# The gate of a mixture-of-experts layer fed with raw rows: deviation and mean applied at the logits, setup and stores reordered

## The reference

```python
logits = x_flat @ Wg + bg                    # x_flat: layernorm(x), 4096 x 512; Wg: 512 x 8
probs = softmax(logits); assignments = argmax(probs)
h = gelu(einsum('nd,edh->neh', x_flat, W1) + b1)
eo = einsum('neh,ehd->ned', h, W2) + b2
out = probs[assignments] * eo[assignments]   # one expert per row
x = x + out
```

## Time and profile before

| | us |
|---|---|
| Median of 3 runs | 2038.52 (2037.73 to 2043.76) |
| Profiled execution, its own time | 2036.4 |
| Its span in the trace | 2034.7 |
| PE busy over the span | 1882.0 (92%) |
| Attention stages | about 1657 of the span |
| Front of the expert stage, until the first matmul of the loop | 1657 to 1735.5 |
| Loop of 23 tiles, until the last DVE step | 1735.5 to about 2024 |

### The profile page before, as it was taken

The page is one execution under the profiler, slowest core; times in us unless marked ns, Lnnn a source line. Parts: engine busy times, 40 slices in busy tenths (PEclk is TensorE's granted clock), DMA queues, the critical chain, the costliest instruction groups (busy, mean ns, idle before and its releaser), DMA issues. The chain is left out here.

```text
span 2034.7 us, 34889 instructions
## 1 busy us (share of the span) xinstructions
PE 1882.0 (92%) x10942; PEld 1325.2 (65%) x10942; DVE 1342.8 (66%) x2837; ACT 1140.2 (56%) x2179; POOL 1000.9 (49%) x1147
## 2 busy tenths in 40 slices
PE   2999999999999999999999999999999835999997
PEld 2666666767666766656666666666666324898896
DVE  3666676666667676767575757575765335688886
ACT  3455554555555465655565655565655515787885
POOL 3354555455545555445444545555554434345454
PEclk9999999999999999999999999999999967899999
DMA  6444545545454575445454544535443369322220
GB/s 202 105 101 110 123 103 131 120 107 135 109 132 100 124 182 125 110 113 125 105 125 105 119 111 111 119 87 127 91 103 79 74 201 333 121 78 88 79 86 21
DMA packets 138089, 239.96 MB, mean 118 GB/s; under 512 B 31114, under 2 KB 32434, under 8 KB 137872
## 3 DMA queue, kind: packets, MB, share of 16 engines
q1 hardware_dynamic: 105728, 191.00, 34.7%
q0 software_dynamic: 21968, 46.42, 11.6%
q10 hardware_dynamic: 10240, 0.64, 0.3%
HBM read 115.63 MB, written 50.02 MB: 81 GB/s over the span
## 5 line engine op out<-in xcount | busy, mean ns | idle before, releaser
L535 ACT ACTIVATE attn_probs<-attn_sT 128x512 f32<-128x512 f32 (+3 forms) x1024 | 529.1, 519 | 484.5 <-PE attn_sT L826 480.0
L442 POOL TENSOR_TENSOR attn_probs<-attn_probs 128x512 f32<-128x512 f32 (+2 forms) x384 | 531.1, 1401 | 177.0 <-PE attn_o_ps L841 125.7
L641 DVE TENSOR_REDUCE attn_m_col<-attn_sS 128x1 f32<-128x512 f32 x512 | 342.6, 687 | 193.9 <-PE attn_sS L810 186.1
L826 PE MATMUL attn_sT<-attn_stack 98*128 98x512 f32 (+2 forms) x1024 | 387.6, 390 | 2.8 <-ACT attn_probs L535 2.8
L810 PE MATMUL attn_sS<-attn_stack 97*128 97x512 f32 (+2 forms) x1024 | 369.3, 371 | 14.5 <-DVE attn_m_col L641 6.0
L647 DVE CUSTOM_DVE_ANT_0 attn_sS<-attn_sS,attn_cT_low 128x128 f32<-128x128 f32 x496 | 241.2, 504 | 191.1 <-PE attn_sS L810 187.5
L826 PEld LDWEIGHTS attn_sT<-attn_stack 98*128 98x128 f32 x1024 | 188.0, 189 | 210.1 <-ACT attn_probs L535 115.6
L430 POOL TENSOR_SCALAR_AFFINE_SELECT attn_probs<-attn_probs 128x256 f32<-128x256 f32 x256 | 132.0, 516 | 361.7 <-ACT attn_probs L535 361.6
L841 PE MATMUL attn_o_ps<-attn_probs,attn_V 128*32 128x512 f32 (+3 forms) x2048 | 233.5, 527 | 24.3 <-POOL attn_probs L430 19.6
L810 PEld LDWEIGHTS attn_sS<-attn_stack 97*128 97x128 f32 x1024 | 193.9, 190 | 70.1 <-DVE attn_m_col L641 18.3
L790 PE MATMUL attn_pj<-attn_xT_high,attn_w_high 128*128 128x512 f32 x384 | 153.1, 399 | 3.9 <-DVE attn_w_low L607 3.9
(11 more groups left out here) (190 smaller groups left out, 3765.0 us busy)
## 6 DMA issues: line engine op xcount, KB each, us to landing
attn_stack<-attn_stage SPq DMA_DIRECT2D x672, 128.0 KB, 2.3
attn_rows<-in_x_dram SPq DMA_DIRECT2D x64, 256.0 KB, 4.0
attn_rows<-x_after_self SPq DMA_DIRECT2D x64, 256.0 KB, 4.2
moe_w<-in_L_ffn_W_dram SPq DMA_DIRECT2D x16, 1024.0 KB, 14.9
attn_stack<-attn_stage POOLq DMA_DIRECT2D x96, 128.0 KB, 3.4
x_after_self<-attn_rows SPq DMA_DIRECT2D x32, 256.0 KB, 2.6
x_after_self<-in_L_attn_b_dense_dram POOLq DMA_DIRECT2D x32, 256.0 KB, 5.0
attn_rows<-in_ctx_dram SPq DMA_DIRECT2D x32, 256.0 KB, 3.0
```

The costliest lines, as they stand in the source:

```text
L442: pool.tensor_tensor(total, total, tile_of(n, kb)[:, js, q0:S], ALU.add).then_inc(added, 1)
L535: act.activation(tile_of(n, kb)[:, j, q0:S], sT[:, i % 2, q0:S], ACT.Exp, scale=SCALE).then_inc(exp_done, 1)
L641: dve.tensor_reduce(to, sS[:, k % 2], AX_X, ALU.max).then_inc(s_free, 1)
L826: pe.matmul(sT[:, i % 2, q0:S], stack[0:ROW_MAX + 1, n % 2, 1, j, kb * P:(kb + 1) * P], stack[0:ROW_MAX + 1, n % 2, 0, j, q0:S], start=Tru ...
```

## The change

It touches only the expert stage. Five things are done:

1. PE transposes raw rows as soon as a batch is loaded; `normalize_batch` on ACT and POOL's normalizing of tiles 2 and 3 are gone. Since logits = ((x @ Wg) - mean * sum(Wg)) / deviation + bg, PE once multiplies a matrix of ones by the gate's weights (column sums, `gate_sums`), POOL forms `-mean/deviation * gate_sums + bg` for each batch (`shift`, two steps of 128x32, two batches late), and DVE multiplies the logits by 1/deviation and adds that (one more step in `choose`).
2. POOL's clearing of the gather buffers (`rows`) and its two selects on `carry` move from behind the first batch's layernorm to ahead of it.
3. ACT's order after the last batch is new: all four `store_rec` come ahead of ACT's steps for the route, the first right behind `take_gate` of batch 7. DVE runs `weigh(0)` ahead of `choose(2)`.
4. SP waits for the first tile's gather before it issues the first three loads of b2.
5. SP also waits for DVE's statistics (`g_stats`) before it overwrites a batch.

The diff, cut to its core:

```diff
@@ sync @@
                     if e >= NB:
                         sp.wait_ge(g_full, NB * (2 * (e - NB) + m + 1))
+                        sp.wait_ge(g_stats, N_STATS * (2 * (e - NB) + m) + NB)
...
+            sp.wait_ge(gathered[0], 16 * R)
             for i in range(RING):
                 tile(0, i)
             sp.wait_ge(placed, 4)
             sp.wait_ge(loaded[weight_sem[LENT]], 16)
-            sp.wait_ge(gathered[0], 16 * R)
             load_weights(LENT)
@@ gpsimd @@
+            pool.memset(ones, 1.0).then_inc(const_step, 1)
...
-                for t in range(NB):
-                    if t not in ON_ACT:
-                        pool.tensor_scalar(gx[b][:, t], gx[b][:, t], rec_tok[:, NB * b + t, 1:2],
-                                           rec_tok[:, NB * b + t, 2:3], ALU.mult, ALU.add).then_inc(g_norm[1], 1)
-
-            layernorm(0)
+            def shift(b):
+                ts = slice(NB * b, NB * (b + 1))
+                pool.wait_ge(g_ln, 4 * b + 4)
+                pool.wait_ge(sums_ready, 1)
+                pool.tensor_tensor(logits[:, ts], gate_sums.unsqueeze(1).broadcast_to([P, NB, E]),
+                                   rec_tok[:, ts, 2].unsqueeze(2).broadcast_to([P, NB, E]), ALU.mult).then_inc(shifted, 1)
+                pool.wait_ge(shifted, 2 * b + 1)
+                pool.tensor_tensor(logits[:, ts], logits[:, ts], bg_rows.unsqueeze(1).broadcast_to([P, NB, E]),
+                                   ALU.add).then_inc(shifted, 1)
+
+            pool.memset(rows[:], 0.0).then_inc(const_step, 1)
             pool.wait_ge(route, 4)
             for c in range(2):
                 pool.affine_select(out=carry[:, c, 0:NT], ...)
-            pool.memset(rows[:], 0.0).then_inc(const_step, 1)
-            for b in range(1, B):
+            for b in range(B):
                 layernorm(b)
+                if b >= 2:
+                    shift(b - 2)
+            shift(B - 2)
+            shift(B - 1)
@@ scalar @@
-            normalize_batch(0)
             for b in range(B):
                 take_turned(b, 0)
                 take_turned(b, 1)
-                if b + 1 < B:
-                    normalize_batch(b + 1)
                 if b >= 1:
                     take_gate(b - 1)
                 take_turned(b, 2)
...
                 take_turned(b, 3)
-            for i in range(PAIRS - 1):
-                exponent(i)
+                if b == B - 1:
+                    exponent(0)
+            exponent(1)
             take_gate(B - 1)
+            store_rec(0)
+            exponent(2)
+            store_rec(1)
             exponent(PAIRS - 1)
-            for i in range(2):
+            for i in range(2, PAIRS):
                 store_rec(i)
...
-            for i in range(2, PAIRS):
-                store_rec(i)
@@ vector @@
                 dve.wait_ge(g_gate, 2 * (2 * i + 1) + 2)
+                dve.wait_ge(shifted, 2 * (2 * i + 2))
                 for b in range(2 * i, 2 * i + 2):
-                    op = dve.tensor_tensor(logits[:, NB * b:NB * (b + 1)],
-                                           logits_back(b).rearrange("p (t c) -> p t c", t=NB)[:, :, 0:E],
-                                           over_tiles(bg_rows, NB), ALU.add)
+                    op = dve.tensor_tensor(cand[:, bs], logits_back(b).rearrange("p (t c) -> p t c", t=NB)[:, :, 0:E],
+                                           over_experts(rec_tok[:, bs, 1]), ALU.mult)
                 step(op)
+                stepped()
+                step(dve.tensor_tensor(logits[:, ts], logits[:, ts], cand[:, ts], ALU.add))
...
+            weigh(0)
             choose(2)
             spread_counts(0)
-            for i in range(PAIRS - 1):
+            for i in range(1, PAIRS - 1):
                 weigh(i)
@@ tensor @@
             def turn(b, t):
-                wait_normed(pe, b, t)
+                pe.wait_ge(loaded[b], 16)
...
-                if b == 0:
+                if b == 1:
                     pe.wait_ge(const_loaded, 16 * 3)
                     pe.transpose(b1_bank, b1_rows, ident[0:E * KT, 0:E * KT])
+                    for k in range(KT):
+                        pe.matmul(sums_bank, ones, wg[:, k, 0:E], start=k == 0, stop=k == KT - 1)
```

More of the change, by code:

```diff
@@ L973, in expert_layer @@
         same = take(E)
+        ones = take(P)
+        gate_sums = take(E)
         numbers_i = take(N_NUMBERS, I32)
@@ L1000, in expert_layer @@
         b1_bank = hidden[:, 3, 0:E * KT]
+        sums_bank = hidden[:, 3, 2 * P:2 * P + E]
         def logits_back(b):
@@ L1009, in expert_layer @@
         loaded = sems("loaded", B)
-        g_stats, g_ln, g_norm, g_full = sem("g_stats"), sem("g_ln"), [sem("g_norm_act"), sem("g_norm_pool")], sem("g_full")
+        g_stats, g_ln, g_full = sem("g_stats"), sem("g_ln"), sem("g_full")
+        sums_ready, shifted, carried = sem("sums_ready"), sem("shifted"), sem("carried")
         g_copied, g_gate, lg_copied = sem("g_copied"), sem("g_gate"), sem("lg_copied")
@@ L1026, in expert_layer @@
         out_tokens = x_out.rearrange("b s d -> (b s) d")
-        N_CONST = 16
+        N_CONST = 17
         N_STATS = 2 * NB
-        ON_ACT = (0, 1)
         weight_sem = {e: 2 * (e % NB) + (1 if e < NB else 0) for e in range(E)}
@@ L1034, in wait_weights @@
             eng.wait_ge(loaded[weight_sem[e]], 16 * 3)
[L1036 to L1040, removed]
         @block.sync
@@ L1130, in _ @@
                 pool.affine_select(out=carry[:, c, 0:NT], in_=carry[:, c, 0:NT], compare_op=ALU.is_ge, fill=0.0,
-                                   base=-1 - P * c, pattern=[[E, NT], [0, E]], channel_multiplier=-1)
-            pool.memset(rows[:], 0.0).then_inc(const_step, 1)
-            for b in range(1, B):
+                                   base=-1 - P * c, pattern=[[E, NT], [0, E]], channel_multiplier=-1).then_inc(carried, 1)
+            for b in range(B):
                 layernorm(b)
+                if b == 2:
+                    pool.wait_ge(const_loaded, 16 * 3)
+                if b >= 2:
+                    shift(b - 2)
+            shift(B - 2)
+            shift(B - 1)
             pool.wait_ge(rec_stored, 16 * PAIRS)
@@ L1177, in _ @@
             act.dma_start(bg_rows, bg.partition_broadcast(P)).then_inc(const_loaded, 16)
-            def normalize_batch(b):
-                act.wait_ge(g_ln, 4 * (b + 1))
-                for t in ON_ACT:
-                    act.activation(gx[b][:, t], gx[b][:, t], ACT.Identity, scale=rec_tok[:, NB * b + t, 1:2],
-                                   bias=rec_tok[:, NB * b + t, 2:3]).then_inc(g_norm[0], 1)
             def take_turned(b, t):
@@ L1216, in _ @@
                 take_turned(b, 2)
-                if b == 0:
+                if b == 1:
                     act.copy(b1_cols[:].rearrange("p e k -> p (e k)"), b1_bank)
+                    act.copy(gate_sums, sums_bank).then_inc(sums_ready, 1)
                 take_turned(b, 3)
-            for i in range(PAIRS - 1):
-                exponent(i)
+                if b == B - 1:
+                    exponent(0)
+            exponent(1)
             take_gate(B - 1)
+            store_rec(0)
+            exponent(2)
+            store_rec(1)
             exponent(PAIRS - 1)
-            for i in range(2):
+            for i in range(2, PAIRS):
                 store_rec(i)
@@ L1350, in spread_counts @@
                 dve.tensor_copy(spread[:, c], totals[c].broadcast_to([P, P])).then_inc(spread_ready, 1)
-            dve.wait_ge(const_step, 13)
+            dve.wait_ge(const_step, 14)
             step(dve.tensor_copy(numbers, numbers_i))
@@ L1496, in turn_back @@
                 pe.transpose(logits_back(b), lgT[b % 2], ident[:]).then_inc(g_gate, 1)
-            pe.wait_ge(const_step, 12)
+            pe.wait_ge(const_step, 13)
             for b in range(B):
@@ L1514, in _ @@
             pe.wait_ge(const_step, N_CONST)
+            pe.wait_ge(carried, 2)
             for c in range(2):
```

7 lines of the change are left out of this document (3 added, 4 removed).

## The result

| | before | after |
|---|---|---|
| Median of 8 runs each, in turns on one chip | 2039.03 us (2035.56 to 2048.69) | 2032.18 us (2028.80 to 2034.37) |
| Ratio after / before | | 0.9956, 95% interval 0.9936 to 0.9976 |
| Profiled execution, own time (span) | 2036.4 us (2034.7) | 2031.96 us (2030.2) |

The changed kernel is 0.44% faster by the means (2031.98 against 2040.87 us), which is 9 us with an interval of 5 to 13; the medians lie 6.9 us apart. Three of the eight times of the kernel before are above 2043 us; without them its mean would be 2037.5, 5.5 us over that of the changed kernel. But the likeliest case of the prediction, 72%, was a gain too small to tell, and the gain can be told: the size of the gain was forecast too small.

The account below looks back on a forecast made before the run. The first gather was taken to wait for 16-byte stores going packet against packet with expert weights. Stores 3.3 plus b2 1.1 gave 4.4 us off 2036.4, so 2032.0, or 2034.1 on the median's scale; range 2031.0 to 2037.5.

Parts of the forecast that it names:

- The bound: Before the loop: the first gather waits for the 16-byte stores, 3.8 us later than the route, slowed by expert weight packets.
- Rival 1: Stores aren't held by the weights; the table of places decides, 13.0 us gained, 2023.4 or 2025.5 us; chance 10%.
- PE's start and period: Gate: PE begins at 1662.6 instead of 1668.33, period 3.24 instead of 3.52 us; last transposes end 11 us earlier.
- The stores: ACT's queue: first packet at 1696.2, 22.4 us of packets one against one with weights, landed at 1720.6; 3.3 us gained.
- The sum: Whole kernel: 3.3 + 1.1 = 4.4 us gained, profiled execution 2032.0, on the median's scale 2034.1.
- POOL's new steps: Gate: two added 128x32 steps a batch at 0.3 us each; POOL needs 2.6 us a batch, hidden behind DVE.
- rival 2: POOL's new steps cost 1.40 us each, delaying stores 1 to 3; 1.7 us gained in all, 2034.7 or 2036.8; chance 15%.
- The table: Route: table of places ready 10.2 us earlier, at 1709.9, there by 1711, 9 us ahead of the stores.
- ACT held until 46.9 in the stage: Issuing the last stores holds ACT until 1704.0, ahead of its route steps, at most 1 us too late for PE.
- b2 behind the gather: First gather: b2's three loads no longer run beside it; 1.1 us gained, possibly nothing or 1 us lost.
- The setup: POOL's clearing and two selects, 3.8 us, move to its wait for first statistics; no gain beyond raw rows.
- Rival 3: PE stays at half clock in the whole gate; gather 6.9 us later, 2042.2 or 2044.3 us; chance 5%.

Follow-up runs that it names:

- `after_held`: Changed kernel with the six weight arrays of experts 5 to 7 issued behind the first gather instead of in the front; 2024.03 us, ratio 0.9931 to the kernel before.
- `before_held`: Kernel before the change with the six weight arrays of experts 5 to 7 issued behind the first gather; 2035.58 us, ratio 0.9990.

## Why the prediction was right and wrong

**The bound.** Right. The stores hold the gather in both kernels, by packets that go one against one; with the weights gone the table holds it (`after_held`). Rival 1, that the weights don't hold the stores, fell: POOL waited 27.2 us for the stores with the table ready.

**PE's start and period.** The start was right, 5.6 for 5.5 us. The period was forecast as 3.52 less the one wait of 0.28, 3.24 us, and is 3.02. The wait of 0.28 counts from the modelled end of the transposes ahead of it, 1.09 us after their start; when nothing waits, the next matmul starts 0.93 us after it, within that end, and the turning back takes 0.11 us of the period instead of 0.17. Here a stop cost PE more than the wait in the row, 0.50 us for 0.28. Seven periods of 0.22 are 1.5 us. The clock rose 4.3 us after the start instead of 5.5, which is 0.6 us more in this trace; the column sums cost 1.06, at the upper bound, and not 0.4, which takes 0.7 back. The sum, last transposes at 32.0 for 33.2, is the first half of the step that failed.

**The stores.** The forecast was 3.8 us from the issue to the first packet, 22.4 us of packets and 2.0 to land. In the trace of after the first packet went 3.9 us after the issue, at 1700.3. Nearly all were gone at 1722.0, 21.7 us later, as the count of 4160 gives, but stragglers went until 1723.5, 23.2 us after the first, and the stores had landed at 1723.82, only 0.3 us behind the last packet. So they end 1.3 us earlier by their start, 0.8 later by the stragglers and 1.7 earlier by the landing: 61.3 us in the stage for 63.5. The landing of 2.0 us was read where packets went at several hundred a us until the end; in the four traces of before it is 1.1 to 1.9, in those of after, with few packets at the end, 0.3 to 0.4. That is 5.5 us between these two traces; the mean of four before is 0.4 below the one from which I had worked, and that of after 0.1 above its first, which leaves 4.9 us of gain where **3.3** were forecast. That is the term that was mis-sized, by 1.6 us, all of it in one direction. The prediction had it in its bounds (1.5 us either way, and a sixth of the forecast's chance on more than 1.7), but the chance was too low: it took the wait that it saw in the period and no smaller ones, and it added a landing read behind a burst to an end without one.

**The sum.** It lacks one more thing. The forecast took 4.4 us off one execution and put that on the median's scale. Four executions of each kernel differ by 6.6 us in the stage, and the timed ratios by 9 us, with an interval of 5 to 13. The remaining 2.4 us are within the spread ahead of the stage, in which nothing was changed, and no run here assigns them.

**Other steps.** POOL's new steps at 0.3 us: 0.25, so rival 2 fell. The table at 52.8 to 53.9: 51.9. ACT held until 46.9 in the stage: 45.5. b2 behind the gather, 1.1 us: 1.2 to 1.3, shown from both sides. The setup, no gain beyond raw rows: right. Rival 3, half clock in all of the gate, fell: PE was at full speed 3.0 to 5.2 us after its start. The loop as long as before: right within the spread.

**The Trainium skill** (DMA: Bandwidth & Descriptors, Queues, rings and completion order) says that an engine goes round the queues which have work, a packet at a time. The traces agree on the turns, with 386 against 386. As to size, 16 against 16 in 0.086 us on 16 engines is one descriptor of 2 KB against one of 16 bytes; turns of several would not come out even in so short a stretch, and in the 24 such stretches from 1710 to 1712 there are 16 to 19 of each.

## What to carry to other kernels

A small transfer that shares the DMA engines with a bulk load is paid in turns, not in bytes: 4096 stores of 16 bytes last as long as 4096 packets of the bulk load. Bringing the first store forward by 14.9 us brought their landing forward by 4.9 only, since packets that had gone alone behind the bulk now go in turns with it. Taking some bulk away (two of eight experts) brought the gather forward by another 6.9. Bulk that is put off should be through before the next transfers that a tile waits for: in one trace each, the same four arrays cost the loop nothing in one piece and 6 us when spread between tiles. When a wait goes from an engine's stream, take the period from rows that follow each other without a stop, not from the old period less the wait seen.

## What the runs showed of the hardware

- Two busy queues shared the DMA engines one packet for one packet, 2 KB against 16 bytes: 381 to 380, 386 to 386 in 2 us, 16 to 16 in 0.086 us. A 16-byte packet takes little of the engine itself (386 of them a share of 10.9% beside 98.3% for as many of 2 KB); without weights they go at 2130 in 2 us.
- An engine that issues DMAs behind a backlog of its own is held with them: ACT stood 5.0, 7.7 and 11.6 us in the issue of stores, and whatever stands behind in its stream waits too. In `before_held`, where the first two stores had gone, the issue of the last two took 1.00 us.
- A DMA of 1024 stores of 16 bytes had its first packet 3.8 to 3.9 us after the issue. The stores had landed 1.1 to 1.9 us after the last packet in the traces of before, which end at several hundred packets a us, and 0.3 to 0.4 us after it in those of after, which end with stragglers.
- A scatter and the gather behind it took 7.25 and 6.86 us beside weight loads, 2.77 and 3.62 without.
- The same attention code ends anywhere within 15 us in 18 executions, and in one pair of them PE's granted clock in a stretch of 60 us was 0.90 and 0.73. The 15 us are more than twice what this change brings to the stage.
